# A graph layer on Trainium2: narrower one-hots for the dense tiles, their weights moved to ScalarE, and smaller side edits

## The reference

```python
xn = layernorm(x)
deg_out, deg_in = segment_sum(w, src), segment_sum(w, dst)
norm = w * rsqrt(deg_out[src] * deg_in[dst] + 1e-12)
h6 = relu(segment_sum((xn @ W6)[src] * norm, dst) + b6)     # pass one over the edges
h7 = relu(segment_sum((h6 @ W7)[src] * norm, dst) + b7)     # pass two over the edges
gnn = h7 @ Wp + bp
k, v = heads(xn @ wk.T), heads(xn @ wv.T)                   # 4 heads of 64
k, v = layer_norm(k) * g + b, layer_norm(v) * g + b         # within a head
mix = (q @ (k.T @ v / N)) @ wo.T + bo
x = x + gnn + mix
x = x + expert_ffn(layernorm(x))
```

## Time and profile before

| | us |
|---|---|
| median of 3 runs | 3923.15 (3919.55 to 3930.97) |
| span of the profiled execution, first to last instruction | 3561.3 |
| time of the profiled execution itself | not recorded |
| median of the runs less that span | 361.9 |
| first gather of pass one, last, first of pass two | 449.2, 1910.2, 1933.3 |
| mean granted TensorE clock | 0.905 |

### The profile page before, as it was taken

The page is one execution under the profiler, slowest core; times in us unless marked ns, Lnnn a source line. Parts: engine busy times, 40 slices in busy tenths (PEclk is TensorE's granted clock), DMA queues, the critical chain, the costliest instruction groups (busy, mean ns, idle before and its releaser), DMA issues.

```text
span 3561.3 us, 51404 instructions
## 1 busy us (share of the span) xinstructions
PE 2813.0 (79%) x15774; PEld 1830.9 (51%) x15774; DVE 1936.5 (54%) x5283; ACT 950.0 (27%) x3210; POOL 2357.1 (66%) x2283
## 2 busy tenths in 40 slices
PE   4565558998989889998953577888778868869998
PEld 4454425555556555655521345555546535545666
DVE  9999846787778777877752142222243242232334
ACT  6787642332333323332220020000020010012111
POOL 5776577777777777777765777777777777730000
PEclk8788979999999999999975799999989999989999
DMA  4110035555555555555555546566646646642221
GB/s 132 59 44 1 2 104 151 167 159 151 162 164 158 150 157 170 155 156 160 166 177 156 170 149 195 197 201 200 195 147 196 197 153 193 198 156 95 79 71 49
DMA packets 260757, 511.33 MB, mean 144 GB/s; under 512 B 64843, under 2 KB 138459, under 8 KB 260141
## 3 DMA queue, kind: packets, MB, share of 16 engines
q0 software_dynamic: 97920, 268.62, 26.0%
q1 hardware_dynamic: 156057, 232.90, 19.7%
q10 hardware_dynamic: 6500, 6.40, 0.5%
HBM read 398.63 MB, written 109.15 MB: 143 GB/s over the span
## 4 chain that ended last, share of the span: by engine, by line
POOL 32%; PE 25%; DVE 15%; issue 12%; DMA 10%; SPq 4%; DVEq 1%; ACT 1%; ACTq 0%; POOLq 0%
POOL ringb L1908 31%; PE ps L676 7%; DVE ab L1058 6%; PE ps L845 5%; PE ps L858 5%; DMA ringb<-t,src 4%; PE ps L653 3%; DVE ab L1056 3%; DMA ab<-in_x 2%; SPq L1969 2%; PE ps L637 2%; SPq L1964 1%; DMA ab<-ad 1%; DMA rsd_in<-rdi 1%; POOL ab L1881 1%
## 5 line engine op out<-in xcount | busy, mean ns | idle before, releaser
L1908 POOL DMA_INDIRECT ringb<-t,src x2040 | 2044.2, 1002 | 684.0 <-issue 604.2
L676 PE MATMUL ps<-xb,ab 125*128 125x256 f32 (+1 forms) x4100 | 1062.0, 399 | 23.0 <-DMA ab<-ad 20.9
L676 PEld LDWEIGHTS ps<-xb,ab 125*128 125x128 f32 x4100 | 796.6, 199 | 287.1 <-issue 103.1
L653 PE MATMUL ps<-mlb 128*125 128x350 f32 x1176 | 495.6, 512 | 127.8 <-DVE mlb L1250 82.5
L637 PE MATMUL ps<-ringb,Sb 128*32 128x257 f32 (+1 forms) x4080 | 348.8, 416 | 280.6 <-DMA ringb<-t,src 178.2
L1697 ACT ACTIVATE ab<-ps 125x300 f32 x637 | 284.3, 446 | 671.0 <-PE ps L653 617.1
L559 PE MATMUL ps<-ab 128*50 128x125 f32 x3240 | 245.9, 306 | 183.3 <-ACT ab L1624 127.6
L1881 POOL TENSOR_TENSOR ab<-ab,wn 128x100 f32<-128x100 f32 x202 | 276.4, 1374 | 126.4 <-DVE ab L1056 126.4
L653 PEld LDWEIGHTS ps<-mlb 128*125 128x125 f32 x1176 | 208.6, 201 | 281.7 <-DVE mlb L1250 163.7
L637 PEld LDWEIGHTS ps<-ringb,Sb 128*32 128x32 f32 x4080 | 83.3, 111 | 496.7 <-DMA ringb<-t,src 273.7
L559 PEld LDWEIGHTS ps<-ab 128*50 128x50 f32 x3240 | 207.8, 143 | 221.2 <-DVE ab L1058 189.2
(11 more groups left out here) (231 smaller groups left out, 2520.8 us busy)
## 6 DMA issues: line engine op xcount, KB each, us to landing
ad<-ab SPq DMA_DIRECT2D x200, 312.5 KB
ab<-ad SPq DMA_DIRECT2D x200, 312.5 KB
ringb<-t,src POOLq DMA_INDIRECT x2040
x2t<-mlb SPq DMA_DIRECT2D x13, 500.0 KB, 18.5
xb<-x2t SPq DMA_DIRECT2D x13, 500.0 KB, 8.2
xb<-in_x SPq DMA_DIRECT2D x10, 625.0 KB
t<-xb SPq DMA_DIRECT2D x10, 625.0 KB
kvb<-t SPq DMA_DIRECT2D x50, 125.0 KB
```

The costliest lines, as they stand in the source:

```text
L653: e.matmul(PS[(2, 7, 4, 5)[bank_of(t)]][0:R, 0:HR], low[:, slot_of(t), :], high[:, slot_of(t), :], start=True, stop=True).then_inc(s_bld, 1)
L676: ins = e.matmul(PS[3][:, 0:wd], lhs, X[0:R, k, 0:wd], start=k == 0, stop=k == NT - 1)
L1908: e.indirect_dma_start(msg[:, slot * QT + k, 0:width], None, table, bass.IndirectOffsetOnAxis(src[:, t:t + 1], 0)).then_inc(s_g[slot], 16)
```

## The change

1. RT goes from 7 to 6: a dense tile may touch six nodes, `Mb` has 300 columns a tile instead of 350, the eviction 5 columns a block instead of 6.
2. The low one-hots of all tiles of a step are one compare (`is_equal`) of 125 columns a tile on VectorE, without the weight. The weight is multiplied in on ScalarE, tile by tile, by the new `weigh_lo(s + 1)`, which runs in step s between the first eviction and the others.
3. The key/value weights are centred once, before pass one: from each head's 64 columns the mean is taken away, so that keys and values come out of PE already centred. The three instructions that did that per tile go; squares and the product with the reciprocal root read PSUM; a tile takes four steps instead of five.
4. The degree becomes the third part of the ring on all partitions: PE broadcasts the degree column as 128 weight columns, and one addition over three parts replaces the two. `s_dad` goes.

```diff
-RT = 7
+RT = 6
...
+KV = 4
...
+        acc3 = accb[:, :].rearrange("p (h n) -> p h n", h=3)
...
                 if L == 0:
-                    e.matmul(bank[0:1, 2 * P:3 * P], ag[:, D:D + 1], ident[:, :], start=True, stop=True)
+                    e.matmul(bank[:, 2 * P:3 * P], ag[:, D:D + 1].to_broadcast([P, P]), ident[:, :], start=True, stop=True)
...
+            heads = wkv.rearrange("p h (a d) -> p (h a) d", d=64)
+            means = h8.rearrange("p a b -> p (a b)")[:, 0:16]
+            e.tensor_reduce(means, heads, AX.X, ALU.add).then_inc(s_cen, 1)
+            e.wait_ge(s_cen, 1)
+            e.tensor_scalar(means, means, 1.0 / 64, None, ALU.mult).then_inc(s_cen, 1)
+            e.wait_ge(s_cen, 2)
+            e.tensor_tensor(heads, heads, means.unsqueeze(2).to_broadcast([P, 16, 64]), ALU.subtract).then_inc(s_cen, 1)
+            e.wait_ge(s_cen, 3)
...
                 if ph == 2:
-                    e.wait_ge(s_kmm, i + 1)
-                    e.tensor_reduce(h8[0:R, 0, :], ps3, AX.X, ALU.add).then_inc(s_kv, 1)
-                    e.wait_ge(s_kv, 8 * i + 1)
-                    e.tensor_scalar(h8[0:R, 0, :], h8[0:R, 0, :], 1.0 / 64, None, ALU.mult).then_inc(s_kv, 1)
-                    e.wait_ge(s_kv, 8 * i + 2)
-                    if i >= 1:
-                        e.wait_ge(s_kk, i)
-                    e.tensor_tensor(kk, ps3, h8[0:R, 0, :].unsqueeze(2).to_broadcast([R, 8, 64]),
-                                    ALU.subtract).then_inc(s_kv, 1)
...
-                    e.tensor_tensor(kk, kk, h8[0:R, 3, :].unsqueeze(2).to_broadcast([R, 8, 64]),
+                    e.wait_ge(s_kv, 5 * i + 2)
+                    if i >= 1:
+                        e.wait_ge(s_kk, i)
+                    e.tensor_tensor(kk, ps3, h8[0:R, 3, :].unsqueeze(2).to_broadcast([R, 8, 64]),
                                     ALU.mult).then_inc(s_kv, 1)
...
-                e.memset(acc[:, :, c0:c0 + R], 0.0).then_inc(s_hz, 1)
-                e.memset(degr[:, c0:c0 + R], 0.0).then_inc(s_hz, 1)
-                freed[0] += 2
+                e.memset(acc3[:, :, c0:c0 + R], 0.0).then_inc(s_hz, 1)
+                freed[0] += 1
...
-                    o = acc[:, :, bass.ds(b, W)]
-                    e.tensor_tensor(o, o, bank[:, 0:2 * P].rearrange("p (h c) -> p h c", h=2)[:, :, j * W:(j + 1) * W],
+                    o = (acc if L else acc3)[:, :, bass.ds(b, W)]
+                    e.tensor_tensor(o, o, bank[:, 0:n * P].rearrange("p (h c) -> p h c", h=n)[:, :, j * W:(j + 1) * W],
                                     ALU.add).then_inc(s_add, 1)
-                    if L == 0:
-                        if added[0]:
-                            e.wait_ge(s_dad, added[0])
-                        o = degr[:, bass.ds(b, W)]
-                        e.tensor_tensor(o, o, bank[0:1, 2 * P + j * W:2 * P + (j + 1) * W], ALU.add).then_inc(s_dad, 1)
...
-                for k in range(n):
-                    e.tensor_scalar(Lb[:, o + k, :], iof[:, 0:R], srcf[:, c0 + k:c0 + k + 1], wn[:, c0 + k:c0 + k + 1],
-                                    ALU.is_equal, ALU.mult).then_inc(s_L, 1)
+                e.tensor_tensor(Lb[:, o:o + n, :], iof[:, 0:R].unsqueeze(1).to_broadcast([P, n, R]),
+                                srcf[:, c0:c0 + n].unsqueeze(2).to_broadcast([P, n, R]), ALU.is_equal).then_inc(s_lo, 1)
...
+            def weigh_lo(s):
+
+                b = BUILD_AT[0].get(s)
+                if not b:
+                    return
+                e.wait_ge(s_lo, batches_before(s) + 1)
+                for k, t in enumerate(b):
+                    row = Lb[:, s % 2 * MLS + k, :]
+                    e.activation(row, row, ACT.Copy, scale=wn[:, TS + t:TS + t + 1]).then_inc(s_L, 1)
...
-                    for t in BUILD_AT[0].get(s, ()):
+                    for t in BUILD_AT[0].get(s, ())[:1]:
+                        evict(t)
+                    weigh_lo(s + 1)
+                    for t in BUILD_AT[0].get(s, ())[1:]:
                         evict(t)
```

More of the change, by code:

```diff
@@ L192 @@
 STEPS0 = max(max(HID_AT) + 2, LAST + 1)
-KV_STEPS = NT * 5
+KV_STEPS = NT * KV
 LATE_AT = FIRST + max(KV_STEPS + 2, DY * PD - 4)
@@ L433, in gnn_block @@
         s_g = [sem(f"s_g{i}") for i in range(RQ)]
-        s_eq, s_S, s_mm, s_cp, s_tr, s_add, s_dad, s_pass = (
-            sem(k) for k in ("s_eq", "s_S", "s_mm", "s_cp", "s_tr", "s_add", "s_dad", "s_pass"))
-        s_xs, s_M, s_L, s_az, s_bld, s_ev, s_c0, s_r0, s_mul, s_lc, s_tc = (
-            sem(k) for k in ("s_xs", "s_M", "s_L", "s_az", "s_bld", "s_ev", "s_c0", "s_r0", "s_mul", "s_lc", "s_tc"))
+        s_eq, s_S, s_mm, s_cp, s_tr, s_add, s_pass = (
+            sem(k) for k in ("s_eq", "s_S", "s_mm", "s_cp", "s_tr", "s_add", "s_pass"))
+        s_xs, s_M, s_lo, s_L, s_az, s_bld, s_ev, s_c0, s_r0, s_mul, s_lc, s_tc = (
+            sem(k) for k in ("s_xs", "s_M", "s_lo", "s_L", "s_az", "s_bld", "s_ev", "s_c0", "s_r0", "s_mul", "s_lc", "s_tc"))
         l_as = [sem("l_as0"), sem("l_as1")]
@@ L469, in kv_copied @@
         def kv_copied(s):
-            return min(max((s - FIRST) // 5 + 1, 0), NT)
+            return min(max((s - FIRST) // KV + 1, 0), NT)
         def hidden_issued(s):
@@ L594, in kv @@
                     e.wait_ge(s_kxc, i + 1)
+                    if i == 0:
+                        e.wait_ge(s_cen, 3)
                     if i >= 1:
-                        e.wait_ge(s_kv, 8 * i - 5)
+                        e.wait_ge(s_kv, 5 * i - 2)
                     for h in range(2):
@@ L683, in dense_turn @@
                 if L == 0:
-                    e.matmul(bank[0:1, 2 * P:3 * P], agd[:, D:D + 1], ident[:, :], start=True, stop=True)
+                    e.matmul(bank[:, 2 * P:3 * P], agd[:, D:D + 1].to_broadcast([P, P]), ident[:, :], start=True, stop=True)
                 for h in range(2):
@@ L1132, in merge @@
                 m = merged[0]
-                merged[0] += 4
-                spill = acc[:, :, CR:CR + SP_]
+                merged[0] += 2
+                spill = acc3[:, :, CR:CR + SP_]
                 e.wait_ge(s_add, added[0])
-                e.tensor_tensor(acc[:, :, 0:SP_], acc[:, :, 0:SP_], spill, ALU.add).then_inc(s_mrg, 1)
-                e.wait_ge(s_dad, added[0])
-                e.tensor_tensor(degr[:, 0:SP_], degr[:, 0:SP_], degr[:, CR:CR + SP_], ALU.add).then_inc(s_mrg, 1)
+                e.tensor_tensor(acc3[:, :, 0:SP_], acc3[:, :, 0:SP_], spill, ALU.add).then_inc(s_mrg, 1)
+                e.wait_ge(s_mrg, m + 1)
+                e.memset(spill, 0.0).then_inc(s_mrg, 1)
                 e.wait_ge(s_mrg, m + 2)
-                e.memset(spill, 0.0).then_inc(s_mrg, 1)
-                e.memset(degr[:, CR:CR + SP_], 0.0).then_inc(s_mrg, 1)
-                e.wait_ge(s_mrg, m + 4)
             merged, added, freed = [0], [0], [1]
@@ L1231, in add_chunk @@
                 e.wait_ge(s_tc, L * ND + d + 1)
-                o = acc[:, :, bass.ds(b, P)]
-                e.tensor_tensor(o, o, PS[3][:, 0:2 * P].rearrange("p (h c) -> p h c", h=2),
-                                ALU.add).then_inc(s_add, 1)
-                if L == 0:
-                    if added[0]:
-                        e.wait_ge(s_dad, added[0])
-                    o = degr[:, bass.ds(b, P)]
-                    e.tensor_tensor(o, o, PS[3][0:1, 2 * P:3 * P], ALU.add).then_inc(s_dad, 1)
+                o, n = (acc if L else acc3)[:, :, bass.ds(b, P)], 2 if L else 3
+                e.tensor_tensor(o, o, PS[3][:, 0:n * P].rearrange("p (h c) -> p h c", h=n), ALU.add).then_inc(s_add, 1)
                 added[0] += 1
@@ L1645, in kv @@
                                  ACT.Copy).then_inc(s_kxc, 1)
+                if ph == 1:
+                    e.wait_ge(s_kmm, i + 1)
+                    e.activation(sq[0:R, :], PS[5][0:R, :], ACT.Square).then_inc(s_ksq, 1)
                 if ph == 2:
-                    e.wait_ge(s_kv, 8 * i + 3)
-                    e.activation(sq[0:R, :], kvs[0:R, :], ACT.Square).then_inc(s_ksq, 1)
-                if ph == 3:
-                    e.wait_ge(s_kv, 8 * i + 4)
+                    e.wait_ge(s_kv, 5 * i + 1)
                     e.activation(h8[0:R, 2, :], h8[0:R, 1, :], ACT.Sqrt, bias=eps5[0:R, :], scale=1.0 / 64).then_inc(s_ksq, 1)
@@ L1759, in act_program @@
                     tile_columns.load(group)
+                weigh_lo(0)
                 for s in range(STEPS0):
```

30 lines of the change are left out of this document (13 added, 17 removed).

## The result

The changed kernel took 3938.12 us (median of 8 runs, 3925.45 to 3953.45), the kernel before 3921.45 beside it (8 runs, 3915.10 to 3930.97): ratio 1.0045, interval 1.0025 to 1.0066. It is slower by 0.45% (0.25% at the least, by the interval), where 3900 us and "faster" were forecast. 3938 lies inside the range of 3879 to 3954; the direction is wrong.

A forecast was written before the change was run, and what follows sets the result against it. POOL's back-to-back gathers were taken to bound both passes. Gathers -13.7, pass two -1, tail -1 and stall -7 gave -22.7 us, from 3923.15 to 3900 us; range 3879 to 3954.

The forecast's parts named there:

- The step that failed: Base of the sum: the profiled span of 3561.3 us, with the 361.9 us up to the median kept as is.
- The second step: PE's dense builds wait about 0.45 us a step more for ScalarE's weighing: nothing, against 0.75 us of cover.
- low compares: New VectorE compares of 250 and 375 columns, with two SBUF inputs, delay gathers in pass one: +9.8 us.
- L1123, now from PSUM: This key/value product on VectorE reads PSUM and so no longer delays gathers in pass one: -5.8 us.
- the stall: POOL's 13.58 us wait late in pass one, behind VectorE's clearing of rows, shrinks: -7 us, bounds 0 and -13.6.
- Six nodes a tile: VectorE's high one-hot compares, 300 instead of 350 columns a tile, delay gathers less in pass one: -17.9 us.
- The first rival: POOL issues no gather between the two VectorE compares, which delay gathers as one: +31 us, 3954 us, chance 0.10.
- Centring the weights: Three new VectorE instructions before its first step, about 2.8 us, run before the first gathers: nothing.
- Pass two: 72 compares of 300 instead of 350 columns delay gathers less in the second pass: -1 us.
- The tail between the passes: After pass one's last gather, four one-row additions and two memsets fewer: -1 us.
- The second rival: ScalarE's weighing and a held-back eviction, in series on PE's path, exceed its cover: +143, about 4043 us, chance 0.07.
- The third rival: Lighter VectorE waits for gathers more often, so compares hit more gathers: -9 us, 3914 us, chance 0.23.

The follow-up runs named there:

- again: The kernel before, unchanged, profiled once more: its run took 3953.91 us with a span of 3952.1.
- p2_late: The changed kernel with ScalarE's weighing placed after all evictions of the step: ratio 1.0087 to the kernel before.
- after_b: The changed kernel, no edit, run again in a set where the kernel before took 3564.79 us: 3546.17 us, ratio 0.9948.
- p2_early: The changed kernel with ScalarE's weighing placed ahead of all evictions of the step: 3616.6 us, ratio 1.0143 to the kernel before.

## Why the prediction was wrong, point by point

**The step that failed** is what bounds the timed runs, and it went in with the base of the sum: "its own full time is not in the record, and the median of the runs, 3923.15, lies 361.9 above that span. I keep this difference." Wherever both are recorded a run is 1.8 or 1.9 us longer than its span, and 3.0 once at the most. The 361.9 us were inside the timed executions' spans, as stops of PE (348 us on issue in `again`, against 8) and as 194 us more of its busy time, less what its other waits shrank by. With that, "POOL issues one gather after another through both passes" did not hold for what was timed: on the upper level POOL waits some 480 us. The whole of the -22.7 is gathers shortened and POOL relieved; on the upper level only *tile* gained anything (11 us), and it lightens PE's builds as well. That a median exceeds a profiled span by 10% was in the table, and I should have asked where it lies and made a rival of it.

**The second step**, false only on the upper level: "I cost this at nothing: 165 + 29 us over 260 building steps is a cover of 0.75 us a step." With PE stopping, there is no such cover. That *low* costs time there is shown: alone it gave 1.0022 and 1.0028, and undoing it takes the loss away (0.9997 and 0.9982). That it costs by one-hots that come late through ACT is argued, from the waits above (58.7 to 106.1 us at the builds with *low* alone; 68.5 to 144.1 for the weights with `p2_late`). The station itself was also priced too low: 0.28 us a tile was worked out from rows that read PSUM, and L1697 took 394 to 397 ns. And what *low* and *keys* save on DVE and the gathers has no price there: the gathers' busy time in pass one fell from 1101.3 (`again`) to 1089.6 us (the changed kernel) and the pass did not shorten (1657 to 1661 us, two sets). Why *keys* alone loses 0.17% was not tested further.

**The steps that held, on the lower level** (`after_b` against the profile before; excess of delayed gathers over 0.947 us in pass one, each put to the DVE instruction that ends 0.82 us before the gather does):

| pass one | before | forecast | `after_b` |
|---|---|---|---|
| high compares, us (gathers) | 72.5 (169) | 55.2 | 53.8 (147) |
| low compares | - | 10.2 | 5.9 (31) |
| L1123, now from PSUM | 6.2 (32) | 0 | 0 |
| busy time of the 1080 gathers | 1119.9 | 1106 | 1102 |
| POOL's wait in the stall | 13.6 | 6.6 | 7.0 |
| POOL's wait for PE | 18.2 | 18 or less | 13.9 |
| pass one, first start to last end | 1462.0 | 1441 (-13.7, -7) | 1437.8 |

- *Six nodes a tile* returned 18.7 us on the gathers (forecast 17.9 x 1.04). The new compares take 776 and 1086 ns (forecast 774 and 1086).
- *The low compares* take 413 and 544 ns (forecast 409 and 539) but cost 5.9 us, not 10.2: after a gather delayed by the first compare, POOL has just issued one when the second runs. The first rival ("two compares act as one") is out. Timeline of `after_b`:

```profile
1069.90 1.08 DVE L1237 TENSOR_TENSOR mlb<-iof,rel 128x900 f32<-128x900 f32 x1
1069.95 1.85 POOL L1908 DMA_INDIRECT ringb<-t,src  x1 [0.30 <-issue]
...
1070.90 0.54 DVE L1239 TENSOR_TENSOR mlb<-iof,src 128x375 f32<-128x375 f32 x1
```

The gather ends at 1071.80, 0.82 after the first compare (1070.98) and 0.36 after the second. The Trainium skill (SBUF — State Buffer, section "Who interferes with whom") infers that descriptor generation is not held up by tensor_tensor; by that rule narrower compares return nothing. The row disagrees, 1.85 us for a gather of 0.95, and so does the table.
- *Centring the weights* was put at nothing. It brings DVE to its first compare 1.4 us later (449.16 instead of 447.75), under the first gather, which took 2.83 us instead of 1.19 (the maximum in the source view above). It is 2.58 to 2.93 us in all eight traces with centred weights and 1.19 to 1.26 in the other twelve: 1.6 us here, once.
- *The stall*: the clearing still waited for stores, 17.4 instead of 22.1 us, and POOL stood 7.0 us. The middle of the two bounds was right.
- *Pass two* was 8 us longer (1222.1 to 1230.5, forecast -1). POOL's wait for PE rose by 10.7 us there, to 28.2, while PE waits for reloads of `A` (L678 behind `ab<-ad`, 26.3 us, against 20.9 before). POOL's wait was 14.3 to 24.8 us in three other traces of that level and 27.6 in `p2_early`, which has the same edits; whether it is scatter between executions or the change stays open. The tail between the passes gave 1.3 us for a forecast of 1.
- *The second rival* (ACT's order becomes the loop): not with the change's order on this level (POOL waits 13.9 us for PE), but with the weights ahead of all evictions it does. The sign that the prediction named for it, over 50 us of POOL's waits for PE, can't tell on the upper level: the changed kernel has 126.4 us named and 162.3 unnamed in pass one, and the kernel before (`again`) has 80.6 and 191.9.
- *The third rival* (nothing to measure, since 13 us of the high compares' gain come back): they cost 53.8 us, below the forecast and not 13 above it, and the ratio 0.9948 on the lower level speaks against it.

So the forecast of -22.7 us held in sign and nearly in size for the level from which its rows came (-18.6 measured; the gathers gave more than forecast, pass two gave some of it back), and was wrong in sign for the executions that were timed.

## What to carry to other kernels

Before costing an edit, compare the profiled span with the timed runs: a gap of more than a few us means that the profile is of another kind of execution, and the timed one has to be profiled before any term is summed. Cover ("PE is idle 0.75 us a step, so a later operand costs nothing") is a property of one execution; where PE stopped, as on the upper level, the same edit lost. So an edit that moves work to an idle engine at the price of a longer chain to PE can cost, as it did here. If one version must serve both levels, the narrower tile is the part to keep: alone 0.997 on the upper, with *degree* 0.993 on the lower, where the two were not run apart.

## What the runs showed of the hardware

- One kernel, unchanged, took 3564 to 3565 us on two chips and 3919 to 3951 on four (medians), steadily (15 to 29 runs a set within 0.9%). In the two traces two parts differ: PE's waits on "issue", 348 us against 8, and the busy time of its 15774 matmuls, 3006.9 us against 2813.0, at a granted clock of 0.872 against 0.905. The gathers' median is the same (949 and 947 ns), and so are the instruction queues' packets and bytes. Windows around the stop shown above (the clock is the third number from the end):

```profile
2520.00:2524.00 4.00, 2.73 (x17) 1.80 (x15) 0.00 (x0) 0.00 (x0) 3.08 (x4) 1.00 0.51 140
2524.00:2526.00 2.00, 0.96 (x3) 0.21 (x2) 0.00 (x0) 0.00 (x0) 1.56 (x2) 0.79 0.61 158
2526.00:2530.00 4.00, 3.18 (x8) 2.31 (x8) 0.98 (x6) 0.00 (x0) 1.10 (x2) 0.50 0.52 154
```

PE ran 3 matmul records from 2524 to 2526, after 17 in the 4 us before. Its first stop (1.31 us before 2524.04) fell while the clock was full, and the clock fell to half (1.2 GHz) behind it, so the clock did not start this stop; what it adds is the slower matmuls after it. In the whole trace 208 of 243 stops of over 0.3 us on issue begin at the full clock. What makes PE stop in some sets stays open. Each chip was seen in one set only, so that the level goes with the chip is not shown either.
- Two small memsets on POOL before each of 2040 gathers (122 ns each) cost 41 us in all: the 0.30 us that the profile shows before each gather can hold other work.
- Leaving out a fifth of the dense matmuls took 129 us (lower level) off PE's busy time and not the 227 that their own time came to: the granted clock fell from 0.905 to 0.889, and the mean of those that stayed rose from 399 to 415 ns.
